# Layer 3 attention: one transposing transfer per tile, and q and k from one joint product

## The reference

```
s = einsum('bhid,bhjd->bhij', q * Dh**-0.5, k)          # 16 heads, Dh = 64
gm = max(s, axis=-1)                                    # over all keys
p = where(causal_mask, 0, exp(s - gm))
out = einsum('bhij,bhjd->bhid', p, v) / (sum(p) + EPS)
return out @ Wo + bo                                    # q, k, v = x @ Wq, x @ Wkv
```

## Time and profile before

| | |
|---|---|
| runs | 1985.29 us median of 3 |
| profiled execution | 1990.92 us, span 1989.1 us |
| PE busy | 1724.1 us (87%) |
| DVE busy | 1417.5 us (71%) |
| ACT busy | 1201.9 us (60%) |
| POOL busy | 1121.0 us (56%) |
| first and last transpose issued | at 1032.0 us and 1945.2 us |

### The profile page before, as it was taken

The page is one execution under the profiler, slowest core; times in us unless marked ns, Lnnn a source line. Parts: engine busy times, 40 slices in busy tenths (PEclk is TensorE's granted clock), DMA queues, the critical chain, the costliest instruction groups (busy, mean ns, idle before and its releaser), DMA issues. The chain is left out here.

```text
span 1989.1 us, 30683 instructions
## 1 busy us (share of the span) xinstructions
PE 1724.1 (87%) x10623; PEld 1107.6 (56%) x10623; DVE 1417.5 (71%) x2088; ACT 1201.9 (60%) x2047; POOL 1121.0 (56%) x1025
## 2 busy tenths in 40 slices
PE   6738999999878798968789998998999999999988
PEld 2416777789543476624635555555555555555564
DVE  3756777763455898753278888888888888888883
ACT  5573333346436576443378787777777777877760
POOL 2425555523200674113237888788888878888880
PEclk7668999997789999988899999999999999999999
DMA  1303222221100000004119998999998999999992
GB/s 39 84 21 94 68 82 86 83 67 32 27 14 6 8 1 1 1 23 138 48 32 158 158 157 158 161 160 161 162 161 150 156 154 161 168 164 165 160 162 54
DMA packets 632582, 193.21 MB, mean 97 GB/s; under 512 B 591617, under 2 KB 624146, under 8 KB 632414
## 3 DMA queue, kind: packets, MB, share of 16 engines
q1 hardware_dynamic: 624038, 167.69, 46.7%
q0 software_dynamic: 8224, 23.51, 3.9%
q10 hardware_dynamic: 168, 0.06, 0.0%
HBM read 36.96 MB, written 12.55 MB: 25 GB/s over the span
## 5 line engine op out<-in xcount | busy, mean ns | idle before, releaser
L2883 DVE TENSOR_REDUCE half_max<-scores 128x1 f32<-128x1024 f32 x512 | 614.6, 1218 | 134.4 <-PE scores L2665 128.6
L2582 POOL TENSOR_TENSOR p_low<-p,p_high 128x2048 f16<-128x2048 f32 (+15 forms) x256 | 576.1, 2251 | 152.7 <-ACT p_high L2809 131.4
L2665 PE MATMUL scores<-k_high,q_pair 128*128 128x512 f16 x1024 | 304.6, 379 | 67.6 <-ACT p L2794 63.0
L2794 ACT ACTIVATE p<-scores,exp_bias 128x1024 f32<-128x1024 f32 (+7 forms) x384 | 317.4, 861 | 70.7 <-DVE exp_bias L2888 68.3
L2809 ACT ACTIVATE p_high<-p 128x2048 f16<-128x2048 f32 (+15 forms) x256 | 282.6, 1104 | 40.7 <-DMA pT_high<-p_high 32.4
L2665 PE MATMUL scores<-k_low,q_pair 128*128 128x512 f16 x1024 | 304.9, 379 | 0.0
L2685 PEld LDWEIGHTS scores<-v_pair,pT_high 128*128 128x128 f16 x2176 | 150.5, 98 | 102.6 <-issue 61.3
L2685 PE MATMUL scores<-v_pair,pT_low 128*128 128x129 f16 x2176 | 185.2, 221 | 10.8 <-DMA pT_low<-p_low 10.5
L2685 PE MATMUL scores<-v_pair,pT_high 128*128 128x129 f16 x2176 | 187.1, 221 | 3.5 <-DMA pT_high<-p_high 3.4
L2685 PEld LDWEIGHTS scores<-v_pair,pT_low 128*128 128x128 f16 x2176 | 146.2, 98 | 45.9 <-DMA pT_low<-p_low 14.9
L2665 PEld LDWEIGHTS scores<-k_low,q_pair 128*128 128x128 f16 x1024 | 99.2, 97 | 122.2 <-issue 0.8
(11 more groups left out here) (503 smaller groups left out, 3207.0 us busy)
## 6 DMA issues: line engine op xcount, KB each, us to landing
pT_high<-p_high SPq DMA_TRANSPOSE x256, 3.6
pT_low<-p_low SPq DMA_TRANSPOSE x256, 3.7
slots<-zero_row SPq DMA_DIRECT2D x1, 3036.0 KB, 14.3
slot_rows<-slots SPq DMA_DIRECT2D x23, 132.0 KB, 2.3
slots_out<-expert_out SPq DMA_DIRECT2D x23, 128.0 KB, 1.8
w_up<-in_L_ffn_inter_w_dram SPq DMA_DIRECT2D x1, 2048.0 KB
x_tokens<-in_L_attn_x_dram SPq DMA_DIRECT2D x4, 256.0 KB, 3.5
dispatched<-moe_rows SPq DMA_DIRECT2D x1, 1024.0 KB, 10.9
```

The lines of the kernel that those rows point to most:

```text
L2582: pool.tensor_tensor(flat(pl[:, buf, b0:b0 + n, :]), flat(p32[:, buf, b0:b0 + n, :]), flat(ph[:, buf, b0:b0 + n, :]), ALU.subtract).then_i ...
L2665: mm = pe.matmul(ps[:, b.start + i, :], q, k[:, par, cs(2 * half + i)], start=start, stop=not start)
L2794: act.activation(flat(p32[:, buf, b0 + first:b0 + first + w, :]), flat(ps[:, banks(p, half), :])[:, 0:w * P], ACT.Exp, bias=bias[:, p:p + ...
L2883: dve.tensor_reduce(mx[:, p % 2, half:half + 1], flat(ps[:, b[half], :]), AX.X, ALU.max, negate=True)\
```

## The change

There are three edits, all in `layer3_attention`.

1. The high and low parts of a tile lie side by side in one buffer (`parts`), and SP issues one transpose for both, after the low part is ready (`turn_parts`). ACT's split and POOL's low both wait for the landing of that one transpose four tiles earlier; PE waits once a tile.
2. q and k come from one product: the weights of q and of k stand side by side (`wqk`), so the lower 64 output partitions are q and the upper 64 are k. There are four units a head, in rounds 0 to 3, in place of eight. A column `scales` (SCALE for q, 1 for k) replaces the constant in the copies.
3. What the product no longer doubles is doubled by transfers from one half of the partitions to the other: for each half of the tokens, two transfers for k (`move_k`, into `klh`) and two for q (`move_q`), 64 partitions x 2 KB each, eight a head. `move_q` overwrites the place from which `move_k` reads, and waits for it. PE's first scores of a head wait for `q_moved`.

The scores are now (high, k) then (q, low): `qhl` holds q's high part below and its low part above, `qlh` the other way round, and `klh` holds k's low part below and its high part above. Weight loads are two a head in place of four, at tile 12 in place of 5.

```diff
+ def move_k(at, par, x):
+     wait(sp, qk_low, at(NCH, 2 * x + 2, 1))
+     sp.dma_start(klh[hi, par, half_of(x)], qhl[hi, par, half_of(x)]).then_inc(k_moved, 16)
+     sp.dma_start(klh[lo, par, half_of(x)], qlh[hi, par, half_of(x)]).then_inc(k_moved, 16)
+ def move_q(at, par, x):
+     wait(sp, k_moved, at(64, 32 * x + 32, 1))
+     sp.dma_start(qhl[hi, par, half_of(x)], qlh[lo, par, half_of(x)]).then_inc(q_moved, 16)
+     sp.dma_start(qlh[hi, par, half_of(x)], qhl[lo, par, half_of(x)]).then_inc(q_moved, 16)
- def turn_high(at, p):
-     wait(sp, p_high, at(NT, p + 1))
-     wait(sp, summed, at(PAIRS, p // 2 + 1 - 2))
-     sp.dma_start_transpose(pTh[:, buf, b0:b0 + n, :], flat(ph[:, buf, b0:b0 + n, :]))
- def turn_low(at, p):
+ def turn_parts(at, p):
      wait(sp, p_low, at(NT, p + 1))
-     sp.dma_start_transpose(pTl[:, buf, b0:b0 + n, :], flat(pl[:, buf, b0:b0 + n, :]))
+     wait(sp, summed, at(PAIRS, p // 2 + 1 - 2))
+     sp.dma_start_transpose(parts_T[:, buf, both_of(b0, n), :], flat(parts[:, buf, both_of(b0, n), :]))
  def prologue(at):
      ...
+     for x in range(2):
+         move_k(at, 0, x)
+         move_q(at, 0, x)
  def head(at, par, h, first, last):
      for p in range(NT):
          if not first or p >= 1:
-             turn_low(*shift(at, par, p - 1)[::2])
-         turn_high(at, p)
+             turn_parts(*shift(at, par, p - 1)[::2])
          ...
-         if p == 5 and not last and h + 2 < H:
-             wait(sp, q_raw, at(NCH, NCH))
+         if p in (4, 8) and not last:
+             move_k(at, 1 - par, p // 4 - 1)
+         if p in (6, 10) and not last:
+             move_q(at, 1 - par, (p - 6) // 4)
+         if p == 12 and not last and h + 2 < H:
+             wait(sp, qk_raw, at(NCH, NCH))
              load(h + 2)
  ...
  def scores(at, par, p, half):            # PE
      if p == 0 and half == 1:
-         wait(pe, k_lows, now(NCH, NCH))
-         wait(pe, q_low, now(NCH, 2))
+         wait(pe, q_moved, now(64, 64))
-     for k, start in ((kh2, True), (kl2, False)):
+     for q, start in ((qhl, True), (qlh, False)):
  ...
- act.activation(qs2[:, par, cs(c)], ps[:, b, :], ACT.Copy, scale=SCALE).then_inc(q_high, 1)
+ act.activation(qhl[:, par, cs(u)], ps[:, b, :], ACT.Copy, scale=scales[:]).then_inc(qk_high, 1)
  ...
+ dve.scalar_tensor_tensor(out=qlh[:, par, cs(u)], in0=ps[:, b, :], scalar=scales[:], in1=qhl[:, par, cs(u)],
+                          op0=ALU.mult, op1=ALU.subtract).then_inc(qk_low, 1)
```

More of the change, by code:

```diff
@@ L2394, in layer3_attention @@
     BLOCKS = NT + 1
[L2395 to L2399, removed]
+    lo, hi = slice(0, DH), slice(DH, P)
+    half_of = lambda x: slice(x * TOK // 2, (x + 1) * TOK // 2)
     UBANK, OBANK = 6, 7
@@ L2657, in scores @@
                         if p == 0 and half == 1:
[L2658 to L2663 removed]
+                            wait(pe, q_moved, now(64, 64))
+                        for q, start in ((qhl, True), (qlh, False)):
                             for i in range(2):
[L2665 removed]
+                                mm = pe.matmul(ps[:, b.start + i, :], q[:, par, ORDER[p] * P:(ORDER[p] + 1) * P],
+                                               klh[:, par, cs(2 * half + i)], start=start, stop=not start)
                         mm.then_inc(scored, 1)
@@ L2677, in add_up @@
                             buf, b0, n = place(p)
-                            if b == 0:
-                                wait(pe, (high_turned, low_turned)[part][p % 4], at(16 * PER_SLOT, turns_by(p)))
+                            if b == 0 and part == 0:
+                                wait(pe, turned_parts[p % 4], at(16 * PER_SLOT, turns_by(p)))
                             if (p, part, b) == work[0]:
@@ L2723, in head @@
                                         scores(at, par, 2 * s + 2 + i, half)
-                                    if (i, half) == (0, 0) and not last:
+                                    if (i, half) == (0, 0) and not last and s < NCH:
                                         unit_free(at, s)
@@ L2831, in head @@
                                     split(*shift(at, par, 2 * s + i - 1)[::2])
-                                if i and not last:
+                                if i and not last and s < NCH:
                                     high(at, 1 - par, s, UBANK)
@@ L2837, in prologue @@
                             values_high(u // 2, u % 2, u % 8)
-                        for u in range(len(UNITS)):
+                        act.wait_ge(scales_set, 2)
+                        for u in range(NCH):
                             high(at, 0, u, u % 8)
```

97 lines of the change are left out of this document (41 added, 56 removed).

## The result

The changed kernel takes 1937.94 us (median of 4 runs, 1935.61 to 1941.38), the kernel before beside it 1984.28 (4 runs): ratio 0.9761, 95% interval 0.9739 to 0.9782. The forecast was 1940. The size is right, but the sum behind it is not: it adds up a DMA path that does not set the length of a head, and it meets the measured length by chance, as the experiments show.

What follows compares the result with a forecast made beforehand. SP's issue and the DMA engines were taken to bound the head in turn. 46.7 + 1.0 + 4.9 + 1.0 = 53.6 us, taken as 54.0, saves 48 us over 15 heads, less 3.3 at the start: 1940 us, range 1890 to 1992.

Steps and rivals of the forecast that it cites:

- What bounds the kernel: SP's queue without gaps: 54.5 of a head's 57.2 us; SP's issue and the DMA engines set the head in turn.
- Data at 191 GB/s, 46.7 us: DMA path: a head's 8.91 MB of transposes at the rate of the best long stretch, 46.7 us.
- The moves, 4.9 us a head: DMA queue: eight 128 KB transfers a head at 212 GB/s, 0.62 us each; bounds 0 and 14.4 us.
- The q move's lateness: PE before the next head's first scores: some 1.5 us late with today's queue, about 4 us to spare without it.
- the threshold of 1 us: Sign of a wrong forecast: single moves of over 1 us that hold up the transposes behind them.
- The joint product counted at nothing: PE, ACT and DVE: 4 of 8 products and their copies go, no gain; 3.8 us a head were PE the bound.
- The price of merging, 52.7 us, hidden: Loop over two pairs of tiles, split, low, merged landing, split: 52.7 us a head, just under the DMA path.
- the 3 set as the mark: Sign of the slower case: ACT waiting on landings for more than 3 us a head; chance 0.17.
- Today that head start is worth nothing: High part sent before the low: worth nothing after the first tile, since SP's queue is longer, 7 to 9 us.
- POOL second, at 51.2 to 54.6: POOL's 46.6 us of work plus waits for ACT's splits: next bound of a head, 51.2 to 54.6 us.
- Saving and start: 3.2 us saved in each of 15 heads, 48 us; first scores 3.3 us later; net -44.7 us.
- Marks: Right: SP gaps, about 185 GB/s, landing waits not above today's. Wrong: DMA share 0.93 with 57 us heads, q-move waits.

Runs made afterwards that it cites:

- small tiles alone: Kernel before with one transpose for both parts only for tiles of 1 to 8 blocks, two for bigger ones: 1948.6 us, ratio 0.9817.
- the copies put back: Changed kernel with ACT's copy and DVE's subtraction repeated into a spare tile in rounds 4 to 7, without products: 1950.8 us, ratio 0.9828.
- the joint product alone: Changed kernel with the two transposes a tile of before; one product for q and k and the moves stay: 1973.5 us, ratio 0.9913.
- finish on DVE: Changed kernel with POOL's two finishing operations, the normalization of the output, moved to DVE: 2006.2 us, ratio 1.0114.
- merging alone: Kernel before with one transpose a tile for both parts; eight doubled products as before, no moves: 1956.2 us, ratio 0.9832.
- whole units more: Changed kernel with product, ACT's copy and DVE's subtraction repeated into unused places in rounds 4 to 7: 1957.4 us, ratio 0.9846.

## Why the prediction was right in size, and where its steps failed

- *What bounds the kernel.* Half right. The fixed cost of small issues held the head back (small tiles alone -1.8%). But "the head is set by SP's issue and by the DMA engines in turn" does not hold for the whole head: SP without gaps was a queue that held up pairs 1, 6 and 7 of a head. The other pairs go by the ring of PE, DVE and ACT: the copies put back show it for pairs 5 to 7 and 0, while for 2 to 4 it rests on the waits.
- *Data at 191 GB/s, 46.7 us.* The failed term. I took a stretch with a partly empty queue for the limit. At the 290 of the changed kernel's full stretches the 8.91 MB would need 31 us (8.91 / 0.290, an estimate); the "212 when it is full" holds for most stretches of the kernel before, not for all. Nor does this path set the head: taking 1.05 MB a head out of it changed nothing. That the sum, 53.6, equals the measured 53.6 is chance.
- *The moves, 4.9 us a head.* Measured 0.1 (heads of 53.5 without them): the lower bound of the prediction held. The q move's lateness was foreseen for the old queue, and the kernel with the joint product alone has it. As single rows the moves are 0.58 us, one in the timeline above 1.16: the threshold of 1 us was passed without harm.
- *The joint product counted at nothing.* Failed: 0.7 to 0.9% or 1.2 us a head, of which ACT's and DVE's copies make 0.8. "All three engines have idle time while they wait for the transposes" was wrong: they wait mostly for each other, and work put back on them lengthened the head.
- *The price of merging, 52.7 us, hidden.* Right: ACT's wait for landings is 0.7 us a head (10.1 / 13.95), under the 3 set as the mark. It is hidden because the small tiles are merged; with only the big ones merged ACT waits 82.8 us for landings in 750, and a head takes 59.1. "Today that head start is worth nothing" was wrong for a full queue on SP: with the small tiles apart, giving it up cost 1.9 and 2.3 us a head.
- *POOL second, at 51.2 to 54.6.* Not borne out as a bound of the whole head. It is 88% busy (656.6 of 750), but 4.7 us less on it, with as much more on DVE, bought 0.4 in pairs 0 and 1. Whether POOL, full in pairs 5 to 7, holds them is open, as said above.
- *Saving and start.* Measured 3.6 x 15 = 54 against 48, and 4.9 against 3.3: a move lands 2.4 us after its issue where 1.2 to 2.0 was taken. The sum has no term for the 5.6 us by which the first transpose comes later behind the first scores, nor for the last head, 3.9 us shorter. Without the 4.5 us that were gained ahead of layer 3, the two profiled executions differ by 47.4 us, where 44.7 were forecast. Saving merged 2.4 + joint product 1.2 = 3.6.
- *Marks.* SP has gaps; the rate is 189 GB/s (185 foreseen); POOL no longer waits for landings; PE has no q wait in the loop. The share of 0.92 stayed, and told nothing. The rate follows from the bytes and the length of the head alone, so it does not speak for the path behind the sum.

None of the whole versions beats the changed kernel; taking the early high part back for big tiles is the same within the intervals.

## What to carry to other kernels

A queue without gaps shows that something is queued, not that the queue sets the time everywhere: compare the length of each round between kernels, and those that no change moves belong to another bound. Test the suspected bound by taking work off it; here that cleared the moves' bytes on the DMA engines (a head without them is 0.1 us shorter). Work that is only handed to another engine tests both at once, and cleared nothing for POOL. Merge small transfers first where their fixed cost is the queue, as here (1.18 us of issue for one block), and price freed engine time by the ring the engines form, not by idle time.

## What was not expected of the hardware

- The 1.50 us of the multiply on DVE is a mean of two lengths. In the changed kernel with the finish on DVE, the 40 of its additions and multiplies (128x512 f32) that began while POOL ran no tensor operation took 0.63 to 0.69 us, the 24 that began while it ran one 0.83 to 2.02. On POOL they take 1.28 and 1.05. So the work moved from POOL to DVE cost 4.4 us a head, where its four pieces at 0.66 each would take 2.6 (an estimate from the 0.63 to 0.69 us). Two pieces, and POOL beside the second:

```profile
1357.89 0.69 DVE L2884 TENSOR_TENSOR o_all<-o_raw,den 128x512 f32<-128x512 f32 x1
...
1406.44 1.77 DVE L2884 TENSOR_TENSOR o_all<-o_raw,den 128x512 f32<-128x512 f32 x1
...
1406.11 1.55 POOL L2579 TENSOR_TENSOR p_parts<-p,p_parts 128x640 f16<-128x640 f32 x1 [1.45 <-ACT p_parts L2791]
1407.62 0.90 POOL L2573 TENSOR_TENSOR p<-p,past 128x128 f32<-128x128 f32 x1
```

- ACT's copy with a scale column took 677 ns where the one with a constant took 585. The line's durations (minimum, median, maximum) in the changed kernel:

```profile
L2780 ACT ACTIVATE high_then_q<-scores,qk_scales x64: 668/677/687, 1010.4 to 1804.1; 128x512 f16<-128x512 f32 x64
```

- A full queue moves the transposes at one of two levels, and the level goes with the kernel. In the nine kernels with the joint product it is 278 to 302 GB/s (30 to 44% of the quarter microseconds from 1100 to 1850 us, against 1 to 6% at the other level); in the five without it, 200 to 225 (37 to 50%, against 5 to 8%). Merging does not decide it. The kernel with merging alone in 1416 to 1420.6 us, then the one with whole units more in 1482.2 to 1485.6:

```profile
GB/s 216 220 216 223 196 200 211 227 211 216 216 225 211 220 220 218 218 209 216 227 220 209 216 216 227 209 216 225 220 214 220 218 218 214 216 216 225 216 205 167
```

```profile
GB/s 111 247 286 289 286 289 295 289 289 289 292 289 289 289 292 289 289 289 295 289 289 289 289 289 289 289 295 289 286 289 301 289 289 289 292 286 280 286 289 368
```

Their heads take 54.8 and 54.6 us, so the level is worth little here. Why it differs is open.
